# The usual remaining tiles in the near arm of a two-way branch, a sixth tile turned ahead, and SyncE's requests for tile rows and padding moved forward

## What is computed

```python
x = x + tanh(g_xattn[0]) * xattn(layernorm(x), ctx_1024, Wq, Wkv, Wc)      # x: (8, 512, 256)
x = x + tanh(g_ffn[0])   * ffn(layernorm(x), gate_w, w1, b1, w2, b2)

def ffn(x, ...):                                # 4096 tokens, width 256
    logits = x @ gate_w                         # 8 experts
    top_v, top_i = top_k(logits, 2)
    top_w = softmax(top_v)                      # comb: the two weights at the two experts
    for e in range(8):
        h = gelu(xf @ w1[e] + b1[e])            # 256 -> 1024
        out += comb[:, e] * (h @ w2[e] + b2[e]) # 1024 -> 256
```

## Time and profile before

| | us |
|---|---|
| median of 3 runs | 922.67 (920.38 to 923.02) |
| the profiled execution | 924.47 |
| its span, first to last instruction | 922.6 |
| PE busy in the span | 799.5 (87%) |
| DVE, ACT, POOL busy | 520.1, 370.6, 421.1 |
| chain that ended last: PE, DVE, issue | 67%, 11%, 6% |

### The profile page before, as it was taken

The page is one execution under the profiler, slowest core; times in us unless marked ns, Lnnn a source line. Parts: engine busy times, 40 slices in busy tenths (PEclk is TensorE's granted clock), DMA queues, the critical chain, the costliest instruction groups (busy, mean ns, idle before and its releaser), DMA issues.

```text
span 922.6 us, 20384 instructions
## 1 busy us (share of the span) xinstructions
PE 799.5 (87%) x6326; PEld 545.6 (59%) x6327; DVE 520.1 (56%) x1516; ACT 370.6 (40%) x772; POOL 421.1 (46%) x472
## 2 busy tenths in 40 slices
PE   3765889989799898988776997999999999999985
PEld 1333344535344353434335886899999999998763
DVE  4475666766766667776553764444444544444442
ACT  1221244543637254456672623333333333333331
POOL 4576545565567554535633653333333333333422
PEclk9868799979899798989997998999999999999998
DMA  5553424263343526114253265343333333333310
GB/s 173 134 117 114 82 69 82 92 139 94 94 91 116 104 69 134 62 63 133 89 171 116 65 164 96 55 63 58 55 58 58 62 68 61 60 57 48 59 30 7
DMA packets 74744, 79.84 MB, mean 87 GB/s; under 512 B 12464, under 2 KB 68528, under 8 KB 74672
## 3 DMA queue, kind: packets, MB, share of 16 engines
q1 hardware_dynamic: 61376, 62.00, 26.2%
q0 software_dynamic: 13296, 16.92, 10.9%
HBM read 50.94 MB, written 28.61 MB: 86 GB/s over the span
## 4 chain that ended last, share of the span: by engine, by line
PE 67%; DVE 11%; issue 6%; ACT 6%; POOL 4%; DMA 4%; SPq 1%; DVEq 0%; ACTq 0%; POOLq 0%
PE ps_o L470 10%; PE ps_a L460 10%; PE ps_e L470 9%; PE ps_d L1500 6%; PE ps_o L1580 5%; PE ps_d L460 5%; PE ps_e L460 4%; PE ps_d L1543 3%; PE ps_e L1475 3%; PE ps_e L1605 3%; PE ps_a L1563 2%; DVE row_max L1267 2%; PE ps_e L1458 2%; PE ps_d L451 2%; ACT prob L1111 1%
## 5 line engine op out<-in xcount | busy, mean ns | idle before, releaser
L1111 ACT ACTIVATE prob<-ps_a 128x512 f32<-128x512 f32 x192 | 113.1, 604 | 181.0 <-PE ps_a L1563 108.8
L1267 DVE TENSOR_REDUCE row_max<-ps_d 128x2 f32<-128x384 f32 x237 | 127.7, 550 | 60.9 <-PE ps_d L1543 59.2
L412 DVE TENSOR_TENSOR prob<-hidden 128x512 bf16<-128x512 f32 (+1 forms) x156 | 101.2, 658 | 70.3 <-ACT hidden L375 70.0
L351 POOL DMA_INDIRECT out<-prob,narrow x71 | 112.4, 1584 | 42.4 <-POOL narrow L349 29.5
L460 PE MATMUL ps_a<-x_in,w_split 128*128 128x256 bf16 (+1 forms) x972 | 109.5, 267 | 0.8 <-issue 0.7
L470 PE MATMUL ps_o<-w_split,hidden 128*128 x640 | 106.9, 273 | 2.5 <-DVE prob L422 1.6
L1543 PE MATMUL ps_d<-k_st,w_split 96*128 96x192 bf16 x474 | 84.5, 268 | 25.7 <-DVE row_max L1267 19.2
L347 POOL TENSOR_TENSOR narrow<-narrow,ones_f 128x2 f32<-128x2 f32 (+1 forms) x39 | 7.3, 188 | 213.8 <-DVE prob L426 200.1
L460 PEld LDWEIGHTS ps_a<-x_in,w_split 128*128 x972 | 91.1, 99 | 13.1 <-issue 1.6
L1042 POOL TENSOR_TENSOR w_split<-w_stage,w_split 128x1024 bf16<-128x1024 f32 x32 | 68.0, 2130 | 61.9 <-ACT w_split L1184 61.6
L470 PE MATMUL ps_o<-w_split,prob 128*128 x320 | 87.2, 273 | 0.0
(11 more groups left out here) (246 smaller groups left out, 1335.9 us busy)
## 6 DMA issues: line engine op xcount, KB each, us to landing
w_stage<-w SPq DMA_DIRECT2D x32, 512.0 KB, 3.8
xg<-queue SPq DMA_DIRECT2D x32, 260.0 KB, 2.9
w_split<-q_split SPq DMA_DIRECT2D x24, 256.0 KB, 8.1
wq_sb<-b SPq DMA_DIRECT2D x39, 128.0 KB, 2.9
x_in<-x SPq DMA_DIRECT2D x8, 512.0 KB, 4.0
hidden<-ctx_t SPq DMA_DIRECT2D x8, 512.0 KB, 3.8
x<-x SPq DMA_DIRECT2D x8, 512.0 KB, 4.1
q_split<-hidden SPq DMA_DIRECT2D x16, 256.0 KB, 3.4
```

Source lines behind the costliest of these rows:

```text
L351: pool.indirect_dma_start(k.out_rows, bass.IndirectOffsetOnAxis(ap=m.token_at[:, c:c + 1], axis=0), m.y[s][:, c, :], None, bounds_check=B ...
L412: self.v.tensor_tensor(m.h_lo[s][:, both, rows], m.hidden[s][:, both, rows], m.h_hi[s][:, both, rows], ALU.subtract).then_inc(self.t.h_lo_ ...
L1111: a.activation(prob[n % 2][:, j, :], ps_a[i % 2][:], ACT.Exp, scale=SCALE).then_inc(exp_ready, 1)
L1267: v.tensor_reduce(row_max[:, t, 2 * pair:2 * pair + 2], bank[:, 0:2 * SLOTS].rearrange("p (h r) -> p h r", h=2), AX.X, ALU.max).then_inc(m ...
```

## The change

Three things, on all five engines:

- **Branch.** `in_general` becomes `usual_or_general`. It takes the rest of the tiles as a function `main`, puts it into the arm that directly follows the test (`If(flag < 1)`), and puts the general path, followed by a second copy of `main`, into `Else`. An engine that has run the near arm then leaves it past the far arm.
- **Tile 5 ahead.** Its turn, `split_x` and `prepare` move from behind the branch into the flow, to the first of the four beats of tile 4's second layer (beat 36 of 0 to 39); SP asks for its rows at the end of the flow, directly after its three waits.
- **SP's order.** In stage 8 `early(0)` (rows of tile 2, bias of tile 1, b2 of tile 0) moves from step 5 to step 1, ahead of the weight piece at step 3; `early(1)` from step 18 to 16, ahead of the store of batch 7. In stage 9 the paddings move from step 8 to step 3, ahead of `early(3)` (bias of tile 4, b2 of tile 3) at step 6.

```diff
@@ TileScalar.early
             self.gelu(i, i // 2, i % 2, n, self.m.early_h[(PAIRS * i + n) % 3])
+        elif i == N_EARLY - 1 and n == 0:
+            self.split_x(N_EARLY, N_EARLY % 2)
@@ TileVector.early
+        elif i == N_EARLY - 1 and n == 0:
+            self.prepare(N_EARLY, N_EARLY // 2, N_EARLY % 2)
         elif n == PAIRS - 1:
             self.finish(i, i // 2, i % 2, self.m.ps_y[0])
@@ TileTensor.early
             self.layer2(i, i % 2, self.e[1], n // 2, range(half * (n % 2), half * (n % 2) + half), self.m.ps_y[0])
+            if i == N_EARLY - 1 and n == 0:
+                self.early_turn(N_EARLY)
@@ flow
-        SP_TILE = ((B, 5), (B, 18), (B, 29), (B + 1, 6), (B + 1, 14))
+        SP_TILE = ((B, 1), (B, 16), (B, 29), (B + 1, 6), (B + 1, 14))
-        DVE_PADS, DVE_PARTS, DVE_OWNERS, DVE_EXPERTS, DVE_ROWS, SP_PADS = 1, 2, 5, 8, 11, 8
+        DVE_PADS, DVE_PARTS, DVE_OWNERS, DVE_EXPERTS, DVE_ROWS, SP_PADS = 1, 2, 5, 8, 11, 3
             sp.wait_ge(tables_ready, 2)
+            tiles.rows(N_EARLY, N_EARLY % 2)
@@ experts
-        def in_general(engine, select_all, attend_all, finish, early, clear=()):
+        def usual_or_general(engine, main, select_all, attend_all, finish, early, clear=()):
             flag = engine.value_load(k.wide[0:1, 0:1], min_val=0, max_val=1)
-            with engine.If(flag > 0):
+            with engine.If(flag < 1):
+                main()
+            with engine.Else():
                 engine.drain().then_inc(flow_met, 1)
...
                 engine.wait_ge(early_met, 5)
+                main()
@@ experts, sync
-            loads.rows(N_EARLY, N_EARLY % 2)
-            loads.rows(N_EARLY + 1, 1 - N_EARLY % 2)
-            loads.bias(N_EARLY, N_EARLY % 2)
-            over_tiles(sp, body)
+            def main():
+                loads.rows(N_EARLY + 1, 1 - N_EARLY % 2)
+                loads.bias(N_EARLY, N_EARLY % 2)
+                over_tiles(sp, body)
...
+            usual_or_general(sp, main, general[0].sp, general[1].sp, pad, early)
@@ experts, gpsimd
+            usual_or_general(pool, main, general[0].pool, general[1].pool, None, early, clear=k.spent)
             pool.wait_ge(t.added, adds(N_TILES))
@@ experts, scalar, vector and tensor: main() is over_tiles and the last finish or second layer, without
-            tiles.split_x(N_EARLY, N_EARLY % 2)
-            tiles.prepare(N_EARLY, N_EARLY // 2, N_EARLY % 2)
-            turn(N_EARLY, N_EARLY // 2, N_EARLY % 2)
```

More of the change, by code:

```diff
@@ L2656, in _, with body @@
             usual.sp(sp)
+            loads = TileLoads(sp, k, t)
+            def body(i, half, s, more, two_more):
+                if two_more:
+                    loads.rows(i + 2, s)
+                if more:
+                    loads.bias(i + 1, 1 - s)
+                loads.b2(i, s)
+            def main():
+                loads.rows(N_EARLY + 1, 1 - N_EARLY % 2)
+                loads.bias(N_EARLY, N_EARLY % 2)
+                over_tiles(sp, body)
             def pad():
@@ L2667, in early @@
                     again.early(i)
[L2669 to L2677, removed]
-            loads.rows(N_EARLY, N_EARLY % 2)
-            loads.rows(N_EARLY + 1, 1 - N_EARLY % 2)
-            loads.bias(N_EARLY, N_EARLY % 2)
-            over_tiles(sp, body)
+                again.rows(N_EARLY, N_EARLY % 2)
+            usual_or_general(sp, main, general[0].sp, general[1].sp, pad, early)
         @block.gpsimd
@@ L2686, in _, with main, body @@
             usual.pool(pool)
-            chain = Chain(pool, pool_steps)
+            def main():
+                chain = Chain(pool, pool_steps)
+                tiles = TileAdds(nc, pool, k, t, chain)
+                def body(i, half, s, more, two_more):
+                    tiles.scatter(i, s)
+                    chain.restart()
+                over_tiles(pool, body)
             def early():
+                chain = Chain(pool, pool_steps)
                 again = TileAdds(nc, pool, k, k.tiles_again, chain)
@@ L2732, in _, with main, body @@
             v = nc.vector
-            chain = Chain(dve, dve_steps)
+            def main():
+                chain = Chain(dve, dve_steps)
+                tiles = TileVector(nc, dve, k, t, chain)
+                def body(i, half, s, more, two_more):
+                    chain.restart()
+                    if more:
+                        tiles.prepare(i + 1, half + s, 1 - s)
+                    for n in range(PAIRS):
+                        tiles.h_lo(i, s, n)
+                    if not begins(i, N_EARLY + 1):
+                        tiles.finish(i - 1, half + s - 1, 1 - s, m.ps_y[1 - s])
+                over_tiles(dve, body)
+                tiles.finish(N_TILES - 1, (N_TILES - 1) // 2, (N_TILES - 1) % 2, m.ps_y[(N_TILES - 1) % 2])
             def make_tables():
+                chain = Chain(dve, dve_steps)
                 pad_places(v, chain, k, pads_placed)
@@ L2751, in early @@
                 chain.restart()
[L2753 to L2763, removed]
-            tiles.prepare(N_EARLY, N_EARLY // 2, N_EARLY % 2)
-            over_tiles(dve, body)
-            tiles.finish(N_TILES - 1, (N_TILES - 1) // 2, (N_TILES - 1) % 2, m.ps_y[(N_TILES - 1) % 2])
+            usual_or_general(dve, main, general[0].dve, general[1].dve, make_tables, early)
         @block.tensor
```

39 lines of the change are left out of this document (18 added, 21 removed).

## The result

The changed kernel takes 908.06 us (median of 4 runs, 907.40 to 908.48) beside 922.85 us of the kernel before on the same chip: ratio 0.9845, 95% interval 0.9827 to 0.9863, 14.8 us less. I had forecast 904.3, 18.4 less. The time lies in the range; 3.7 us of the gain are missing.

A forecast was written before the change was run, and what follows sets the result against it. PE was taken to bound the tile loop, so only its idle gaps before it, at tile 2's rows and the branch, could shrink. 10.8 + 8.4 - 0.3 - 0.5 = 18.4 less gave 904.3 us, range 901 to 911.

The forecast's parts named there:

- signs that the prediction names for being wrong: PE idle over 1 us at three named places, issue gap behind test, instruction packets in loop, or POOL's drain late.
- first rival: Batch 7's chain takes PE's place as the limit: PE waits 3.4 at the rows' turn, 907.7; chance 0.15.
- Rows of tile 2 first: Stage 8: earlier request ends PE's 7.06 us wait and its half clock; gain 10.8 us.
- Batch 7's chain, taken as 0: PE's turn of batch 7's rows: PE would wait 0 to 3.4 us for the rows; taken as 0.
- Tile 5 ahead and the near arm: At the branch, tile 4's second layer to tile 5's first: 6.34 us in place of 14.76; gain 8.4.
- three covers: At the branch: tile 5's rows land by 539.9, DVE prepares tile 6 in time, PE's test runs ahead of the array.
- Bias of tile 4: Queued behind the paddings on SP, it lands 2.1 us late for gelu; cost 0 to 2.1, taken as 0.3.
- The jump at the end: Engines leave the near arm over the general path; only POOL's jump, before its drain, costs: 0.5 us.
- The near arm does not stall: Rival: code behind a test must be fetched even without a jump; PE keeps 3.4 us, 907.7; chance 0.08.
- PE's loop stays without instruction packets: Rival: moved loop no longer fits what is held, 3.4 us stop in each of 12 rounds, 945.1; chance 0.05.
- The whole fetch at the end: Rival: POOL's jump waits for its DMA, then fetches; 1.6 more than taken, 905.9, or 907.2; chance 0.10.

The follow-up runs named there:

- u3: Changed kernel with SP's first two turns of tile requests put back to their old steps, behind the weight piece: 915.29 us.
- e6: Changed kernel with ACT's casts of the second, third and fourth of the last four weight pieces at steps 22, 23 and 28 of stage 8: 908.24 us.
- e9: Changed kernel with ACT's casts of the last weight pieces at steps 22 and 26 of stage 8 and 4 of stage 9: 905.65 us.
- e10: Changed kernel with the edits of e5 and e9 together, bias of tile 4 first and the weight pieces later: 904.55 us.
- u4: Changed kernel with the paddings alone put back behind SP's fourth turn of requests, so behind tile 4's bias: 906.70 us.
- e5: Changed kernel with SP asking for tile 4's bias ahead of the paddings instead of behind them: 906.30 us.
- e12: Changed kernel with the old arms for SP, ACT, POOL and DVE, so that PE alone jumps at the end: 907.53 us, one run.

## Why the prediction was right or wrong

The forecast was 18.4 less, and 14.8 came. Two of the signs that the prediction names for being wrong appeared: PE idle over 1 us at the turn of batch 7's rows (2.08) and at tile 4's fourth part (1.21). The time still lies in the range, because its upper end was added up from the bounds of just these terms. That it lies close to the 907.7 of the first rival is luck: this rival has 3.4 lost at the turn, and 1.82 was lost there, with the rest at two other places.

**Rows of tile 2 first: right**, 10.95 for 10.8, with the clock at 1.00 and the request at 475.28 on SP, ahead of the piece. Put back alone (u3) it costs 8.2: the gap itself 8.85, as the clock rose sooner there, while the turn of batch 7's rows waits 1.2 less. So some 2 us of the 10.95 depend on when the clock rises behind such a gap.

**Batch 7's chain, taken as 0: wrong, 1.82.** This is the largest part of the miss. The bound of 0 to 3.4 held it, and the rival "batch 7's chain takes PE's place" named it, but I chose the lower end for a false reason. I had read DVE's low part of 1.98 at 507.85 as late because of gelu, and reckoned that its gelu would move ahead. It was long because of POOL: in the kernel before POOL's low half runs in 507.15 to 509.28, beside it, and other such low parts take 0.69.

```profile
507.15 2.13 POOL L1042 TENSOR_TENSOR w_split<-w_stage,w_split 128x1024 bf16<-128x1024 f32 x1 [0.93 <-ACT w_split L1184]
```

So the cause does not go when PE moves; it meets whichever DVE instruction stands beside the piece, here the shift, 2.03 for 0.15. e6, e9 and e10 show it by taking the piece away; without the meeting the chain takes 4.88 from the moments to the turn (e10, 494.65 to 499.53), near the 4.1 of its members. The Trainium skill says so, which I had not weighed: in "SBUF — State Buffer", section "Who interferes with whom", a DVE instruction with two inputs in SBUF contends with a GpSimd instruction that reads SBUF, and issue order decides who blocks. The traces agree: the shift and the low part of gelu read two tensors in SBUF, began behind POOL's instruction, and end 0.01 (the shift) and 0.55 (the low part, 509.83 beside 509.28) behind its end. DVE's addition at 503.39, which has one input in PSUM, takes its usual 0.69 beside POOL's low halves. Not only instructions with two inputs in SBUF are slowed, though: the scaling behind it (L428), with one tensor in SBUF, takes 2.52 for its two, where one usually takes 0.35.

```profile
501.91 4.39 POOL L1049 TENSOR_TENSOR w_split<-w_stage,w_split 128x1024 bf16<-128x1024 f32 x2 [3.14 <-ACT w_split L1191]
```

```profile
503.39 0.69 DVE L424 TENSOR_TENSOR prob<-ps_o,wq_sb 128x512 f32<-128x512 f32 x1 [4.00 <-PE ps_o L474]
504.19 2.52 DVE L428 TENSOR_SCALAR prob<-prob,narrow 128x256 f32<-128x256 f32 x2
```

**Tile 5 ahead and the near arm: right**, 8.67 for 8.4. Of the three covers, DVE's preparation of tile 6 and the test's load held. For the rows of tile 5 the price was wrong, though on the safe side: they were asked for at 532.57, which is 43.5 after Z, where 536.1 on the clock of the kernel before is 45.0 after Z, since the 9.05 from the earlier trace rows held SP's jump. The sentence that without the paddings' move this would not hold is half right: the rows would be late, but PE would lose only 1.5 us by it, less than the 1.9 that the move costs (u4).

**Bias of tile 4: mechanism right, size off**, 1.88 for 0.3, within the bound of 2.1. I put the landing at 542.4 by the old clock and PE's slack at 1.8; gelu began 2.8 late and not 2.1 (9.32 beside 6.55), and 1.88 of this reached PE, 1.21 and 0.32 of it as waits, so that the slack was nearer 0.9. e5 and u4 take back all of it (1.86 each).

**The jump at the end: size off, and another mechanism**, 0.88 for 0.5. I looked at POOL's own jump ahead of the drain. That one costs nothing: the last DMA of POOL begins at 899.23 and the span ends 6.4 behind it, as before (916.23 and 922.6). What costs is the other engines' jumps, PE's at least (e12), beside the scatter before; I had counted them as free because they end before POOL's drain begins.

**The rivals.** The near arm does not stall (tests of 40 to 93 ns, no gap behind). PE's loop stays without instruction packets in 596 to 815. The whole fetch at the end did not come.

The sum with the measured terms: 10.95 - 1.82 - 1.88 - 0.03 + 8.67 - 0.88 = 15.0.

## What to carry to other kernels

When a gap of PE is closed, follow the next chain instruction by instruction and ask of each long one what ran beside it on the neighbouring engine: a 2 us instruction that is usually 0.7 marks a meeting that can move with the schedule instead of vanishing with its wait. When a request is moved past a jump, take the jump out of its price; when a jump is moved, look at what is in flight at its new place, on the DMA engines too, and not only at the engine that jumps.

## What the runs showed of the hardware

A DVE instruction of 0.15 us took 2.03 because it began 0.10 behind a POOL instruction of 2.12. Jumps to far code at the end of the program lengthen POOL's wait for the landing of a scatter of 128 rows from 1.25 us (three kernels) to between 1.78 and 2.63 (eleven kernels), and the DMA engines' records differ there by the packets of the instruction queues; with PE's jump alone the wait was 1.84. PE's jump over the general path took 4.58 us in one kernel and 5.30 in another with nearly the same general path, and behind the latter PE's granted clock stood at 0.50, 1.2 GHz.
